# A two-layer transformer kernel on one core: its first eight heads' maxima ahead of the pipeline, its last FFN blocks inside the last attention, and GpSimd's residual sums in later steps

## The chip, the core and the metric

The kernel runs on one core of a Trainium2 chip. The metric is the device time of one execution in microseconds (us); lower is better. Five engines work side by side: TensorE (PE, whose weight loads are listed as PEld), VectorE (DVE), ScalarE (ACT), GpSimd (POOL) and SyncE (SP), which here only issues transfers. Each runs its own instruction stream in order, and waits on semaphores that the others raise.

## What is computed

Eight sequences of 256 tokens with width 128 pass two post-norm layers, all in float32:

```python
x = _layernorm(x + _L0_attn_ref(x, Wqkv, bqkv, Wproj, bproj))        # 16 heads of 8, no mask
x = _layernorm(x + _L0_ffn_ref(x, W_exp, ..., down_bias))            # 128 -> 512, butterflies, GELU, 512 -> 128
x = _layernorm(x + _L1_attn_ref(x, Wqa, Wqb, Wkva, Wkvb, Wout, bout))  # 16 heads, 4 key heads, RoPE, causal
x = _layernorm(x + _L1_ffn_ref(x, w_gate, w_up, w_down))             # SiLU-gated, 384 hidden
```

The softmax is taken over 256 keys for each of 256 queries, with the row's maximum subtracted. The butterflies of the first FFN are linear, so the kernel folds them into its two weight matrices once, at the start.

## The kernel before

**Work and numbering.** A batch b is one sequence in one layer: 0 to 7 are the first layer, 8 to 15 the second. Each has 16 heads, so there are 256 heads, m = 16 b + h. All engines walk the same list of steps g = -44, -42, ... 298, two heads a step, and each does in step g what the table of offsets at the top of the file gives it (`AT_PROJ = 26` means: batch b's projection is in step 16 b + 26). The order on every engine is thus fixed by these numbers and by the order of the `if`s in the loop body; nothing is scheduled at run time.

**One head.** A head's scores are computed twice. First `max_scores` (L342) writes queries by keys into one of three PSUM banks `SM`, and DVE takes each row's negative maximum into `mx` (L708; L716 with the mask in the second layer). Every eight heads PE transposes `mx` (L415), ACT copies it to `mt` (L587), and a transfer (L269) puts it into row 31 of the query operand `QK`, whose key side has a row of ones. Then `exp_scores` (L361) computes keys by queries, with the maximum already subtracted, into one of three banks `ST`, and ACT writes the exponentials to `E` (L580). `max_scores` runs `LEAD = 14` heads ahead of `exp_scores`. A head uses 31 or 32 rows of the array; the four strips of 32 rows can work at once. From step -8 to -2 `filler` (L372) takes the place of `exp_scores`.

**The start.** Six matmuls on zeros (L392) come first. Batch 0's operands are made straight into strips by four groups of matmuls (L406, a group r for heads 4r to 4r+3, queries and keys in one of two banks `G`), which ACT copies out with the bias (L610). The groups are in steps -44, -12, -8 and -4 (`FIRST_AT`). Batch 1 is projected in step -10 (L498), copied by ACT (L620), and split into strips by four transfers, issued by ACT's own queue (L626); all later batches' strips are issued by SP (L285). GpSimd builds the folded FFN weights meanwhile (L847 to L864), adds the projection's bias to the residual `xb` (L939), and goes on with the folding.

**The middle.** In a batch's steps follow: values times `E` (L524), DVE's transpose (L805) and reciprocal (L726), GpSimd's product (L885), DVE's transpose (L731), the projection (L468), the residual sum and statistics (L790, L674, L677), GpSimd's LayerNorm (`normalise`: L831, L827, L828, L834), and PE's transpose of its result (L475) into `xt`. In the first layer GpSimd adds the next bias to the normalised tile right behind it, to make the next residual (L916); the same follows the FFN's LayerNorm, for tiles of two batches (L924). The FFN of the first layer takes tiles of two batches, that of the second single batches: `up` (L435, three chunks c), ACT's tanh (L594), DVE's two products (L751, L753), `down` (L457).

**The end.** From step 256 on there are no more scores, and PE may use all eight banks. Batch 14's FFN chunks are in steps 258, 262 and 268, its `down` in 270; batch 15's attention ends with the second half of its values in 260, the projection in 266, LayerNorm in 268 (GpSimd gives the inverse deviation, DVE the rest: L684), transpose in 272; its FFN follows in 274 to 286.

Of the kernel before, what the change touches and what calls it, by code (L numbers as in the profile page):

```python
# [82 lines left out]
def values_at(g):  # L83

    for l in range(2):
        for parity in range(2):
            b = batch_at(g, AT_V[l][parity], (l,))
            if b is not None and b % 2 == parity:
                return b
    return None  # L90
# [20 lines left out]
def block_kernel(nc, x_nat, x_t, ones, wfirst, bfirst, wqk0, wv0, bqk0, bv0, wproj, bproj, u0, d0, fac_u, fac_d, bfw, bup, bcon, bdown,  # L111
# [7 lines left out]
    with ctx:  # L119
# [80 lines left out]
        idle_ready, first_ps, first_out = sem("idle_ready"), sem("first_ps"), sem("first_out")  # L200
# [28 lines left out]
        def layer(b):  # L229
            return b // NB  # L230

# [6 lines left out]
        def _(sp):  # L238
# [26 lines left out]
            for g in STEPS:  # L265
# [7 lines left out]

                if b is not None and b != 1:
# [31 lines left out]
        def _(pe):  # L306
# [18 lines left out]

            def max_scores(m, c):
# [15 lines left out]
                ins = nc.tensor.matmul(SM[m % S_RING][:, cols], q, QK[rows, b % QK_RING, r, 1, keys], start=True, stop=True)  # L342
# [23 lines left out]
            def filler(m, c):  # L366
# [3 lines left out]
                if c == 0 and m >= S_RING - FILL:  # L370
                    pe.wait_ge(filled, m + FILL - S_RING + 1)
# [21 lines left out]

            for g in STEPS:
                scores(g)

                for r in range(GROUPS):
                    if g == FIRST_AT[r]:
                        bank = claim(("first", r), first_out, 2 * (r + 1))
                        if r == 0:  # L400
                            pe.wait_ge(ld["x0"], 16)
                            pe.wait_ge(ld["first"], 32)
                        elif r == 1:
                            pe.wait_ge(ld["groups"], 16)
                        for s in range(2):
                            ins = nc.tensor.matmul(bank[:, s * T:(s + 1) * T], wfirst_sb[:, r, s, :], xt[:, 0:T], start=True, stop=True)  # L406
                        ins.then_inc(first_ps, 1)
# [18 lines left out]
                for c in range(SC):  # L426
                    if (b := batch_at(g, AT_UP1[c], (1,))) is not None:
# [81 lines left out]
                if (n := half_at(g, AT_PV)) is not None:  # L509
# [4 lines left out]
                    else:  # L514
                        pe.wait_ge(A["masked"], 4 * (n - 2 * NB + 1))
                    if t == 0:
                        pe.wait_ge(A["v_ready"], b + 1)
                    for e in range(2):
                        for k in range(QT):
# [44 lines left out]
        def _(act):  # L564
# [5 lines left out]

            for g in STEPS:
# [16 lines left out]
                for c in range(SC):  # L588
                    if (b := batch_at(g, AT_UP1[c], (1,))) is not None:
# [13 lines left out]
                for r in range(GROUPS):  # L603
                    if g == FIRST_AT[r]:

                        act.wait_ge(first_ps, r + 1)
                        if r == 0:
                            act.wait_ge(ld["first"], 32)
                        for s in range(2):
# [470 lines left out]
```

## Time and profile before

| | us |
|---|---|
| median of 3 runs | 374.52 |
| the runs | 372.81, 374.52, 375.20 |
| the profiled execution, its own time | 375.42 |
| its span, first to last instruction | 373.5 |

The profiled execution is 0.9 us above the median, and 1.9 us of it lie outside the span. Mean granted TensorE clock: 0.965 of full speed. Busy shares of the span: PE 91%, its weight loads 63%, DVE 67%, ACT 51%, POOL 48%. PE's share is to be read with care, since matmuls overlap and their ends are modelled; its idle stretches are exact enough, and each names what ended it.

### The profile page before, as it was taken

Reading aid. Unit: us, or ns where it says so; the run is one execution under the profiler, and the core shown is the slowest. Engines: PE = TensorE matmul, PEld = TensorE weight load, DVE = VectorE, ACT = ScalarE, POOL = GpSimd, SP = SyncE. Lnnn points to the kernel's source line nnn. Section 1 sums busy time; section 2 is a strip of 40 time slices with the busy share of each in tenths; the row PEclk is TensorE's granted clock in tenths of the full one; section 3 lists DMA queues with packets and bytes.
Section 4 is the critical chain, followed back from the end, with each engine's and each line's share of the span. In section 5 each row is a group of like instructions: output and inputs, shape, how many; then the busy total and the mean of one; then the engine's idle time right before and its main releaser. Section 6 shows DMA issues by size and latency. Waiting matters only on the chain.

```text
span 373.5 us, 10260 instructions
## 1 busy us (share of the span) xinstructions
PE 340.0 (91%) x3804; PEld 234.7 (63%) x3804; DVE 250.9 (67%) x940; ACT 189.2 (51%) x397; POOL 178.1 (48%) x299
## 2 busy tenths in 40 slices
PE   7879999999999999999999699898999999999672
PEld 3546766666657656576657566586777767676452
DVE  3444667586866777586866668486888898964533
ACT  2123755745585655836575445744556555545100
POOL 5664072140300706046352967339695954637420
PEclk9696999999999999999999989999999999999968
DMA  7321522110011001200202011110112110000000
GB/s 262 125 92 66 75 71 79 31 31 2 3 32 30 4 1 31 47 16 17 46 14 44 4 31 29 33 30 3 32 45 48 29 40 10 18 3 16 16 14 14
DMA packets 9469, 14.27 MB, mean 38 GB/s; under 512 B 2140, under 2 KB 5196, under 8 KB 9292
## 3 DMA queue, kind: packets, MB, share of 16 engines
q1 hardware_dynamic: 8828, 12.83, 13.5%
q10 hardware_dynamic: 592, 0.79, 0.7%
q8 instruction: 30, 0.49, 0.5%
q14 instruction: 19, 0.16, 0.2%
HBM read 6.28 MB, written 1.05 MB: 20 GB/s over the span
## 4 chain that ended last, share of the span: by engine, by line
PE 73%; POOL 9%; issue 6%; ACT 5%; DVE 5%; ACTq 1%; POOLq 0%; DVEq 0%
PE SM L342 26%; PE G L524 10%; PE ST L361 6%; PE G L435 5%; PE G L448 4%; PE G L498 4%; PE G L424 3%; PE G L457 2%; PE G L415 2%; PE G L506 2%; POOL ln_f L834 2%; ACT L580 1%; PE G L468 1%; POOL xb L924 1%; PE ST L392 1%
## 5 line engine op out<-in xcount | busy, mean ns | idle before, releaser
L580 ACT ACTIVATE E<-ST 128x512 f32<-128x512 f32 (+1 forms) x256 | 125.3, 541 | 126.5 <-PE ST L361 126.4
L342 PE MATMUL SM<-QK 31*128 31x256 f32 (+1 forms) x1024 | 146.6, 384 | 8.0 <-ACT QK L610 4.2
L361 PE MATMUL ST<-QK 32*128 32x256 f32 (+1 forms) x1024 | 137.6, 379 | 4.4 <-ACT E L580 4.4
L342 PEld LDWEIGHTS SM<-QK 31*128 31x128 f32 x1024 | 97.7, 189 | 49.0 <-DVE mx L708 13.3
L708 DVE TENSOR_REDUCE mx<-SM 128x2 f32<-128x512 f32 x128 | 82.2, 685 | 44.0 <-PE SM L342 43.6
L361 PEld LDWEIGHTS ST<-QK 32*128 32x128 f32 x1024 | 92.1, 187 | 8.0 <-ACT E L580 6.5
L716 DVE CUSTOM_DVE_ANT_0 masked_s<-SM,mask_sb 128x256 f32<-128x256 f32 (+1 forms) x256 | 75.7, 351 | 23.9 <-PE SM L342 23.3
L885 POOL TENSOR_TENSOR at<-turned,rec 128x256 f32<-128x256 f32 x16 | 10.1, 628 | 94.9 <-DVE rec L726 94.9
L524 PE MATMUL G<-E,V 128*32 128x256 f32 x992 | 53.6, 356 | 0.5 <-POOL E L878 0.5
L878 POOL TENSOR_SCALAR_AFFINE_SELECT E<-E 128x512 f32<-128x512 f32 x64 | 39.0, 634 | 14.0 <-ACT E L580 14.0
L524 PEld LDWEIGHTS G<-E,V 128*32 128x32 f32 x992 | 28.6, 109 | 22.4 <-issue 8.0
L805 DVE STREAM_TRANSPOSE turned<-G 128x256 f32<-128x256 f32 x31 | 13.9, 449 | 16.8 <-PE G L524 16.6
L435 PE MATMUL G<-xt,wf 128*128 128x256 f32 x76 | 21.9, 412 | 0.7 <-ACT xt L599 0.6
L716 DVE DVE_READ_ACCUMULATOR2_ANT mx<- 128x1 f32 x256 | 21.2, 83 | 0.0
L424 PE MATMUL G<-xt,wup 128*128 128x512 f32 x32 | 17.3, 621 | 0.0
L448 PE MATMUL G<-down,hid 128*128 128x128 f32 x128 | 16.3, 281 | 0.1
L435 PEld LDWEIGHTS G<-xt,wf 128*128 128x128 f32 x76 | 13.4, 196 | 4.6 <-ACT xt L599 0.9
L448 PEld LDWEIGHTS G<-down,hid 128*128 128x128 f32 x128 | 15.0, 191 | 1.9 <-issue 0.7
L751 DVE SCALAR_TENSOR_TENSOR gated<-th,G 128x256 f32<-128x256 f32 x19 | 8.0, 420 | 10.0 <-ACT th L594 9.9
L834 POOL TENSOR_SCALAR ln_a<-r_a,nm_a,rstd_a 128x128 f32<-128x128 f32 x30 | 13.2, 447 | 1.6
L415 PE MATMUL G<-id,mx 128*8 128x128 f32 x64 | 12.7, 280 | 0.0
L831 POOL TENSOR_SCALAR nm_a<-mv_a 128x2 f32<-128x2 f32 x15 | 2.9, 191 | 20.2 <-DVE mv_a L677 20.2
(130 smaller groups left out, 427.5 us busy)
## 6 DMA issues: line engine op xcount, KB each, us to landing
QK<-qk SPq DMA_DIRECT2D x56, 64.0 KB
rs<-ry SPq DMA_DIRECT2D x16, 128.0 KB, 2.3
xb<-x_nat SPq DMA_DIRECT2D x1, 1024.0 KB, 4.8
out<-ln_g SPq DMA_DIRECT2D x8, 128.0 KB, 1.9
xt<-x_t SPq DMA_DIRECT2D x1, 896.0 KB, 6.7
wi<-wi_all SPq DMA_DIRECT2D x1, 576.0 KB, 3.8
QK<-mt SPq DMA_DIRECT2D x32, 8.0 KB
fac<-fac_u SPq DMA_DIRECT2D x1, 508.0 KB, 6.4
```

The lines of the kernel that those rows point to most:

```text
L342: ins = nc.tensor.matmul(SM[m % S_RING][:, cols], q, QK[rows, b % QK_RING, r, 1, keys], start=True, stop=True)
L361: ins = nc.tensor.matmul(ST[m % S_RING][:, c * T:(c + 1) * T - q0], QK[rows, b % QK_RING, r, 1, c * P:(c + 1) * P], QK[rows, b % QK_RING, ...
L415: ins = nc.tensor.transpose(bank[0:8, q * P:(q + 1) * P], mx[:, n % 2, q, :], id32[:, :])
L424: nc.tensor.matmul(bank[:, :], wup[:, c * P:(c + 1) * P], xt[:, n * FT:(n + 1) * FT], start=True, stop=True).then_inc(F0["up_ps"], 1)
L435: ins = nc.tensor.matmul(bank[:, s * T:(s + 1) * T], wf[:, s, c * P:(c + 1) * P], xt[:, i * T:(i + 1) * T], start=True, stop=True)
L448: ins = nc.tensor.matmul(bank[:, i * W:(i + 1) * W], hid0[:, c, s * P:(s + 1) * P], down[:, c, :], start=(c == 0), stop=(c == HC - 1))
L524: ins = nc.tensor.matmul(bank[VCOL * j:VCOL * (j + 1), q0:T], values, E[:, (2 * n + e) % E_RING, j, k * T:(k + 1) * T - q0], start=(e == 0 ...
L580: act.activation(E[:, a % E_RING, j, 0:n], ST[m % S_RING][:, 0:n], ACT.Exp, scale=SCALE)\
L708: ins = nc.vector.tensor_reduce(mx[:, n % 2, :, i], bank[:, :].rearrange("p (q k) -> p q k", q=QT), AX.X, ALU.max, negate=True)
L716: ins = nc.vector.tensor_tensor_reduce(out=masked_s[:, m % 2, lo:hi], in0=bank[:, lo:hi], in1=mask_sb[:, T + lo - hi:T], scale=-1.0, scala ...
L834: ins = nc.gpsimd.tensor_scalar(N["ln"][:, parity, s, :], N["r"][:, s, :], N["nm"][:, s:s + 1], N["rstd"][:, s:s + 1], ALU.add, ALU.mult)
L878: nc.gpsimd.affine_select(out=e, in_=e, pattern=[[0, 4], [1, P]], compare_op=ALU.is_ge, fill=0.0, base=0, channel_multiplier=-1).then_inc( ...
```

## The change

It does five things.

1. **Eight heads' maxima ahead of the steps.** `AHEAD = 8`: before the loop over steps PE makes groups 0 and 1, then the maxima of heads 0 to 7, four heads in a run (all their second halves, then all their first halves), then groups 2 and 3. These eight take turns in all six banks, `SM` and `ST`. Group 0's keys go to `ST2`, from where DVE adds the bias, while ACT does the queries. The steps begin at -6, not -44, and the filler has three steps.
2. **Batch 1 and the first values** move to steps -6 and -4; batch 1's strips are issued by SP like the others.
3. **Batch 14's FFN**: PE and ACT have its last chunk in step 264, not 268. DVE has its three chunks in 262, 264 and 268, not 258, 262 and 268, and there the last comes ahead of batch 15's LayerNorm.
4. **Finer waits in batch 15**: `down` starts when two of the three hidden chunks are there, and the last values start when the first of two groups of four heads is masked.
5. **GpSimd's residual sums** leave the LayerNorm: by batch from step 28 to 34 (`AT_XB`), by tile from 74 to 88 (`AT_XB0`).

```diff
+LAST_UP1, LAST_GATED = (34, 38, 40), (38, 40, 44)
+AT_XB, AT_XB0 = 34, 88
-FIRST, FINAL = AT_QK[2], HEADS + 44
+AHEAD = 2 * STRIPS
+FIRST, FINAL = AHEAD - LEAD, HEADS + 44
 STEPS = range(FIRST, FINAL, 2)
-FIRST_AT, EARLY, FILL = (FIRST, -12, -8, -4), (None, -10, 2), 8
+EARLY, EARLY_V, FILL = (None, FIRST, 2), FIRST + 2, 6
...
+def up1_at(g, c, last=LAST_UP1):
+    b = batch_at(g, AT_UP1[c], (1,))
+    return BATCHES - 2 if g - last[c] == H * (BATCHES - 2) else b if b != BATCHES - 2 else None
...
+        keys_bank = ST[S_RING - 1]
+        def max_bank(m):
+            return (SM + ST)[m % (2 * S_RING)] if m < AHEAD else SM[m % S_RING]
...
+            def project_group(r):
+                bank = claim(("first", r), first_out, 2 * r + 1)
...
+                for s in range(2):
+                    to = keys_bank if r == 0 and s == 1 else bank
+                    ins = nc.tensor.matmul(to[:, s * T:(s + 1) * T], wfirst_sb[:, r, s, :], xt[:, 0:T], start=True, stop=True)
+                ins.then_inc(first_ps, 1)
...
                     if b == 0 and j == 0:
-                        pe.wait_ge(first_out, 2 * (r + 1))
+                        pe.wait_ge(first_out, 2 * r + 1)
+                        if r == 0:
+                            pe.wait_ge(first_keys, 1)
...
-                    if m >= S_RING:
+                    if m >= AHEAD:
                         pe.wait_ge(A["max_done"], m - S_RING + 1)
+                    elif m >= 2 * S_RING:
+                        pe.wait_ge(A["max_done"], m - 2 * S_RING + 1)
...
+            project_group(0)
+            project_group(1)
+            for r in range(2):
+                for c in (1, 0):
+                    for m in range(STRIPS * r, STRIPS * (r + 1)):
+                        max_scores(m, c)
+            project_group(2)
+            project_group(3)
...
-                    pe.wait_ge(F1["hid_ready"], SC * (i + 1))
+                    pe.wait_ge(F1["hid_ready"], SC * (i + 1) - (1 if b == BATCHES - 1 else 0))
                     for q in range(QT):
                         for c in range(SC):
+                            if q == 0 and c == SC - 1 and b == BATCHES - 1:
+                                pe.wait_ge(F1["hid_ready"], SC * (i + 1))
...
-                        if b == 1:
-                            act.wait_ge(A["qk_out"], 2)
-                            act.wait_ge(zeros_ready, 1)
-                            for j in range(STRIPS):
-                                act.dma_start(QK[STRIP * j:STRIP * j + ROWS, 1, :, :, :], qk[j:P:STRIPS, 1, :, :]).then_inc(qk_in[1], 16)
...
+            dve.wait_ge(first_ps, 1)
+            dve.wait_ge(ld["first"], 32)
+            nc.vector.tensor_scalar(QK[:, 0, 0, 1, :], keys_bank[:, T:2 * T], bfirst_sb[:, 0, 1:2], None, ALU.add)\
+                .then_inc(first_keys, 1)
+            for m in range(AHEAD):
+                maximum(m)
...
-                    if (b := batch_at(g, AT_UP1[c], (1,))) is not None:
+                    if (b := up1_at(g, c, LAST_GATED)) is not None:
...
+                if g == H * (BATCHES - 1) + AT_LN:
...
+                    normalise_last(NA, b % 2, A["ln_ready"])
...
-                    if layer(b) == 0:
-                        pool.wait_ge(A["ln_ready"], b + 1)
+                if (b := batch_at(g, AT_XB, (0,))) is not None:
+                    pool.wait_ge(A["ln_ready"], b + 1)
...
                     normalise(N0, FS, n % 2, F0["ln_ready"])
+                if (n := tile_at(g, AT_XB0)) is not None:
                     pool.wait_ge(F0["ln_ready"], n + 1)
```

Line numbers in the rows below are those of the file they are from; a row with x2 stands for two instructions of one kind in sequence.

PE at the start, before (groups L406, maxima L342, filler L372, batch 1 L498, transposed maxima L415):

```order
L392 MATMUL ST<-idle 128x512 x3
L406 MATMUL G<-xt,wfirst_sb 128x256 x2
L342 MATMUL SM<-QK 128x256 x8
L406 MATMUL G<-xt,wfirst_sb 128x256 x2
L342 MATMUL SM<-QK 128x256 x4
L498 MATMUL G<-xt,wqk_sb 128x256 x2
...
L406 MATMUL G<-xt,wfirst_sb 128x256 x2
L506 MATMUL G<-wv_sb,xt 128x128 x2
...
L415 MATMUL G<-id,mx 8x128 x2
```

and with the change (groups L356, maxima L379, filler L412, batch 1 L537):

```order
L432 MATMUL ST<-idle 128x512 x3
L356 MATMUL G<-xt,wfirst_sb 128x256
L356 MATMUL ST<-xt,wfirst_sb 128x256
L356 MATMUL G<-xt,wfirst_sb 128x256 x2
L379 MATMUL SM<-QK 128x256 x3
L379 MATMUL ST<-QK 128x256
...
L356 MATMUL G<-xt,wfirst_sb 128x256 x4
L379 MATMUL SM<-QK 128x256 x2
L412 MATMUL ST<-QK 128x256 x2
...
L452 MATMUL G<-id,mx 8x128 x2
L537 MATMUL G<-xt,wqk_sb 128x256 x2
```

All four groups now come before the first filler, the eight heads' maxima stand between the first two and the last two, and batch 1 is behind the transposed maxima instead of ahead of them.

GpSimd at the first tile's LayerNorm, before:

```order
L834 TENSOR_SCALAR ln_f<-r_f,nm_f,rstd_f 128x128 x4
L924 TENSOR_TENSOR xb<-ln_f,bout_sb 128x512
L831 TENSOR_SCALAR nm_a<-mv_a 128x2
L827 TENSOR_SCALAR ve_a<-mv_a 128x2
L828 TENSOR_TENSOR rstd_a<-ve_a,half 128x2
L834 TENSOR_SCALAR ln_a<-r_a,nm_a,rstd_a 128x128 x2
```

and with the change:

```order
L881 TENSOR_SCALAR ln_f<-r_f,nm_f,rstd_f 128x128 x4
L878 TENSOR_SCALAR nm_a<-mv_a 128x2
L874 TENSOR_SCALAR ve_a<-mv_a 128x2
L875 TENSOR_TENSOR rstd_a<-ve_a,half 128x2
L881 TENSOR_SCALAR ln_a<-r_a,nm_a,rstd_a 128x128 x2
L963 TENSOR_TENSOR xb<-ln_a,bcon_sb 128x256
L932 TENSOR_TENSOR at<-turned,rec 128x256
L972 TENSOR_TENSOR xb<-ln_f,bout_sb 128x512
```

The sum of 128x512 has left the place between the two LayerNorms.

DVE from the last values on, before:

```order
L751 SCALAR_TENSOR_TENSOR gated<-th,SM 128x256
L753 TENSOR_TENSOR hid<-SM,gated 128x256
L731 STREAM_TRANSPOSE att<-at 128x256
L790 TENSOR_TENSOR r_a<-ST,xb 128x256
L674 BN_STATS stats_a<-r_a 128x6 x2
L677 BN_AGGR mv_a<-stats_a 128x2 x2
L684 TENSOR_SCALAR ln_a<-r_a,mv_a,rstd_a 128x128 x2
L751 SCALAR_TENSOR_TENSOR gated<-th,ST 128x256
L753 TENSOR_TENSOR hid<-ST,gated 128x256
```

and with the change:

```order
L777 STREAM_TRANSPOSE att<-at 128x256
L797 SCALAR_TENSOR_TENSOR gated<-th,SM 128x256
L799 TENSOR_TENSOR hid<-SM,gated 128x256
L842 TENSOR_TENSOR r_a<-ST,xb 128x256
L710 BN_STATS stats_a<-r_a 128x6 x2
L713 BN_AGGR mv_a<-stats_a 128x2 x2
L797 SCALAR_TENSOR_TENSOR gated<-th,ST 128x256
L799 TENSOR_TENSOR hid<-ST,gated 128x256
L720 TENSOR_SCALAR ln_a<-r_a,mv_a,rstd_a 128x128 x2
```

One pair of products moved behind the transpose `att`, another ahead of `ln_a`. On PE the last chunk's matmuls (before L435 into `ST`) moved ahead of the projection (L468).

## Rows read from the trace of the kernel before

**Rows 1.** Stretches in us: length, then each engine's busy time (instructions), granted clock, DMA.

```profile
12.90:19.60 6.70, 6.23 (x29) 3.78 (x30) 1.40 (x3) 1.25 (x4) 6.20 (x10) 0.50 0.01 3
29.90:36.70 6.80, 6.80 (x41) 4.20 (x38) 3.14 (x7) 2.81 (x7) 4.20 (x1) 0.50 0.00 0
214.20:217.70 3.50, 3.46 (x24) 2.69 (x24) 0.53 (x3) 1.51 (x5) 3.42 (x3) 0.51 0.00 0
357.60:364.40 6.80, 6.24 (x20) 5.07 (x20) 2.00 (x7) 1.15 (x3) 1.96 (x5) 0.50 0.06 19
```

**Rows 2.** PE's timeline, 0 to 46 us: start, length, operation, [idle before <- what ended it].

```profile
22.47 0.48 PE L342 MATMUL SM<-QK 31*128 31x256 f32 x2 [1.39 <-ACT QK L610]
...
23.54 0.38 PE L415 MATMUL G<-id,mx 128*8 128x128 f32 x2
...
31.95 0.80 PE L342 MATMUL SM<-QK 31*128 31x256 f32 x2
...
37.49 1.13 PE L498 MATMUL G<-xt,wqk_sb 128*128 128x256 f32 x4
...
40.72 0.67 PE L342 MATMUL SM<-QK 31*128 31x256 f32 x2
```

**Rows 3.** The timelines of DVE, ACT, SP and GpSimd at the start.

```profile
9.51 1.29 DVE L708 TENSOR_REDUCE mx<-SM 128x2 f32<-128x512 f32 x2 [4.46 <-PE SM L342]
...
7.45 0.84 ACT L610 ACTIVATE QK<-G,bfirst_sb 128x256 f32<-128x256 f32 x2 [3.75 <-PE G L406]
...
18.36 3.17 ACTq L626 DMA_DIRECT2D QK<-qk  x4
...
37.17 2.64 SPq L285 DMA_DIRECT2D QK<-qk  x4
...
32.50 4.51 POOL L939 TENSOR_TENSOR xb<-xb,bproj_sb 128x2048 f32<-128x2048 f32 x1 [7.09 <-DVE bproj_sb L814]
...
59.21 0.63 POOL L885 TENSOR_TENSOR at<-turned,rec 128x256 f32<-128x256 f32 x1 [3.01 <-DVE rec L726]
```

**Rows 4.** DMA activity from 17 to 25 us, in 40 slices of 0.2 us.

```profile
DMA  0000000000000243000433333146300003000000
```

**Rows 5.** GpSimd's sums for the residual, all four tiles and all eight batches.

```profile
L924 POOL TENSOR_TENSOR xb<-ln_f,bout_sb x4: 1264/1266/1273, 124.7 to 254.1; 128x512 f32<-128x512 f32 x4
...
L916 POOL TENSOR_TENSOR xb<-ln_a,bcon_sb x8: 722/730/737, 66.2 to 213.4; 128x256 f32<-128x256 f32 x8
```

**Rows 6.** PE's waits between 46 and 340 us: total us, times, longest.

```profile
PE G L475 <- POOL ln_a L834: 4.8, 4, 2.8
```

**Rows 7.** PE's timeline at the last two of those four waits.

```profile
213.45 0.41 PE L475 MATMUL G<-id,ln_a 128*128 128x128 f32 x2 [2.80 <-POOL ln_a L834]
...
258.91 0.41 PE L475 MATMUL G<-id,ln_a 128*128 128x128 f32 x2 [1.08 <-POOL ln_a L834]
```

**Rows 8.** The page's groups: GpSimd's idle time before its product for the attention.

```profile
L885 POOL TENSOR_TENSOR at<-turned,rec 128x256 f32<-128x256 f32 x16 | 10.1, 628 | 94.9 <-DVE rec L726 94.9
```

**Rows 9.** PE's timeline at the end.

```profile
352.33 0.68 PE L468 MATMUL ST<-wout_sb,att 128*128 128x128 f32 x4 [1.83 <-DVE att L731]
...
356.90 2.31 PE L457 MATMUL ST<-wf,hid 128*128 128x128 f32 x12 [3.02 <-DVE hid L753]
...
366.57 1.57 PE L457 MATMUL SM<-wf,hid 128*128 128x128 f32 x12 [1.48 <-DVE hid L753]
```

**Rows 10.** DVE's timeline at the end.

```profile
350.95 0.42 DVE L751 SCALAR_TENSOR_TENSOR gated<-th,SM 128x256 f32<-128x256 f32 x1 [0.61 <-ACT th L594]
...
351.75 0.43 DVE L731 STREAM_TRANSPOSE att<-at 128x256 f32<-128x256 f32 x1
353.05 0.42 DVE L790 TENSOR_TENSOR r_a<-ST,xb 128x256 f32<-128x256 f32 x1 [0.87 <-PE ST L468]
...
355.37 0.60 DVE L684 TENSOR_SCALAR ln_a<-r_a,mv_a,rstd_a 128x128 f32<-128x128 f32 x2 [1.09 <-POOL rstd_a L828]
...
368.18 0.42 DVE L773 TENSOR_TENSOR r_g<-SM,ln_a 128x256 f32<-128x256 f32 x1 [1.76 <-PE SM L457]
```

More of the change, by code:

```diff
@@ L83, in values_at @@
 def values_at(g):
+    if g == EARLY_V:
+        return 0
     for l in range(2):
@@ L87, in values_at @@
             b = batch_at(g, AT_V[l][parity], (l,))
-            if b is not None and b % 2 == parity:
+            if b and b % 2 == parity:
                 return b
@@ L272, in _ @@
                     b = batch_at(g, AT_QKIN, (1,))
-                if b is not None and b != 1:
+                if b is not None:
                     if layer(b) == 0:
@@ L324, in claim @@
                 return banks[i]
+            def project_group(r):
+                bank = claim(("first", r), first_out, 2 * r + 1)
+                if r == 0:
+                    pe.wait_ge(ld["x0"], 16)
+                    pe.wait_ge(ld["first"], 32)
+                elif r == 1:
+                    pe.wait_ge(ld["groups"], 16)
+                for s in range(2):
+                    to = keys_bank if r == 0 and s == 1 else bank
+                    ins = nc.tensor.matmul(to[:, s * T:(s + 1) * T], wfirst_sb[:, r, s, :], xt[:, 0:T], start=True, stop=True)
+                ins.then_inc(first_ps, 1)
             def max_scores(m, c):
@@ L341, in max_scores @@
                     cols, keys = (slice(T, T + P), slice(0, P)) if c == 0 else (slice(0, T), slice(0, T))
-                ins = nc.tensor.matmul(SM[m % S_RING][:, cols], q, QK[rows, b % QK_RING, r, 1, keys], start=True, stop=True)
+                ins = nc.tensor.matmul(max_bank(m)[:, cols], q, QK[rows, b % QK_RING, r, 1, keys], start=True, stop=True)
                 if c == 0:
@@ L426, in _ @@
                 for c in range(SC):
-                    if (b := batch_at(g, AT_UP1[c], (1,))) is not None:
+                    if (b := up1_at(g, c)) is not None:
                         i = b - NB
@@ L518, in _ @@
                     for e in range(2):
+                        if e == 1 and n == 2 * BATCHES - 1:
+                            pe.wait_ge(A["masked"], 4 * (n - 2 * NB + 1))
                         for k in range(QT):
@@ L569, in _ @@
             act.activation(warm[:, :], half[:, 0:1], ACT.Exp).then_inc(act_chain, 1)
+            for r in range(GROUPS):
+                act.wait_ge(first_ps, r + 1)
+                if r == 0:
+                    act.wait_ge(ld["first"], 32)
+                for s in range(1 if r == 0 else 2):
+                    act.activation(QK[:, 0, r, s, :], g_bank["first", r][:, s * T:(s + 1) * T], ACT.Identity,
+                                   bias=bfirst_sb[:, r, s:s + 1]).then_inc(first_out, 1)
             for g in STEPS:
@@ L588, in _ @@
                 for c in range(SC):
-                    if (b := batch_at(g, AT_UP1[c], (1,))) is not None:
+                    if (b := up1_at(g, c)) is not None:
                         i = SC * (b - NB) + c
@@ L602, in _ @@
                     act.activation(xt[:, n * FT:(n + 1) * FT], g_bank["xt0", n][:, :], ACT.Copy).then_inc(F0["xt_ready"], 1)
[L603 to L609, printed above, removed]
-                            act.activation(QK[:, 0, r, s, :], g_bank["first", r][:, s * T:(s + 1) * T], ACT.Identity,
-                                           bias=bfirst_sb[:, r, s:s + 1]).then_inc(first_out, 1)
                 if (b := projected_at(g)) is not None:
@@ L694, in _, with maximum @@
                 ins.then_inc(v_clean, 1)
+            def maximum(m):
+                b, r, j = place(m)
+                n = m // 8
+                i = 2 * j + r % 2
+                dve.wait_ge(A["sm_ps"], m + 1)
+                if m % 8 == 0 and n >= 2:
+                    dve.wait_ge(A["mt_ps"], n - 1)
+                bank = max_bank(m)
+                if layer(b) == 0:
+                    ins = nc.vector.tensor_reduce(mx[:, n % 2, :, i], bank[:, :].rearrange("p (q k) -> p q k", q=QT),
+                                                  AX.X, ALU.max, negate=True)
+                else:
+                    if m == NB * H:
+                        dve.wait_ge(ld["rope"], 48)
+                    if m >= NB * H + 2:
+                        dve.wait_ge(A["max_done"], m - 1)
+                    for q, lo, hi in ((1, 0, T), (0, T, T + P)):
+                        ins = nc.vector.tensor_tensor_reduce(
+                            out=masked_s[:, m % 2, lo:hi], in0=bank[:, lo:hi], in1=mask_sb[:, T + lo - hi:T], scale=-1.0,
+                            scalar=3.0e38, op0=ALU.add, op1=ALU.min, accum_out=mx[:, n % 2, q, i:i + 1])
+                ins.then_inc(A["max_done"], 1)
@@ L719, in _ @@
-                    ins.then_inc(A["max_done"], 1)
+                    if m < HEADS:
+                        maximum(m)
                 if (b := batch_at(g, AT_NORM)) is not None:
```

64 lines of the change are left out of this document (17 added, 47 removed).

## The prediction

> **What bounds the kernel.** I read the clock by stretches first, then each engine's timeline at both ends, then PE's waits in the middle. PE is busy for 91% of the span, and between 46 and 340 us it hardly waits, so a microsecond comes off only where PE idles or runs at half clock, or where work is taken from its stream. The granted clock is at its lower level (0.50, 1.2 GHz) in four stretches, 23.8 us together [rows 1]: two at the start, one at 214 us, one at the end. Each follows a time in which PE kept stopping: the one at 214 us stands right behind the wait of 2.80 us [rows 7], the last behind waits of 1.83 and 3.02 us [rows 9]. In the middle PE's largest wait is for GpSimd's `ln_a`, 4.8 us in four places [rows 6].
>
> **The front end.** Before, the first operands begin to leave PSUM at 7.45, the first maximum starts at 9.51 [rows 3], the first eight maxima are transposed only at 23.54, step 2 starts at 31.95 and step 8 at 40.72 [rows 2]. What spreads this out is order: four groups, each followed by a round trip through ACT, in four different steps.
> Now with the change, at full clock:
> - Group 1 follows group 0 at once. Two matmuls of 256 columns on the full array take 1.07 us (37.49 with 1.13, less the overlap) [rows 2], so PE is free for maxima at 8.5. That ACT and DVE share group 0's copies saves half of 0.84 [rows 3], but PE doesn't get there before 8.5, so it is worth nothing.
> - A step's eight score matmuls over four strips take 1.07 (22.47 to 23.54) [rows 2]. Sixteen, in runs of four strips, take 2.1; the first head is whole at about 9.4. DVE's two maxima take 1.29 [rows 3], so eight take 5.2: the last ends at 14.6. Groups 2 and 3 (2.1) and ACT's copies lie under that. PE makes step -6's scores meanwhile and transposes the maxima at about 14.9, 8.6 earlier than before.
> - Batch 1: its two matmuls end at 16.3, ACT's copies at 17.2 (0.84). PE goes on with three steps' scores (3.2), the values (0.5) and the bias product (0.4), and stands before step 2 at 20.4. **Here is a new wait.** Step 2 begins with batch 1's first maxima, hence with its strips. SP needs 2.64 for four issues [rows 3], so the last ends at 19.85. In the trace ACT's last issue ended at 21.53 [rows 3] and the activity of these transfers at about 22.8 [rows 4]: 1.3 later. So the strips are there at 21.15; PE waits 0.75 and all of its queue with it. Before, this was hidden: 22.8 against a use at 31.95.
>
> The Trainium skill ("DMA: Bandwidth & Descriptors", the two cost components of a transfer) states a fixed cost of about 2.0 us instead; by it the strips would land at 21.85 and the front end would gain 0.7 less.
>
> - So step 2 starts at 21.2 instead of 31.95. From step 2 to 8 the old kernel needed 8.77, of which 4.75 at half clock (until 36.70 [rows 1]); at full clock 6.4. Step 8 would start at 27.6: **13.1 earlier**.
> - But PE still stops (for the copies, for DVE, for the strips), and half clock came twice in this part of the old trace, 6.7 and 6.8 us long [rows 1]. A stretch costs half its length, 3.3. None gives 13.1, one 9.8, two 6.5. I take one: the stops are fewer, not gone.
> - What else must keep pace? GpSimd's folding ran until 25.4 and then idled 7.09 for `bproj` [rows 3]; that now comes at about 21, so its 4.5 us sum starts at 25.4, 7.1 earlier. At batch 0's product it waited another 3.01 [rows 3]. Together 10.1 us of slack for a shift of 9.8. SP's loads are tied to the steps and move along. I count nothing, with 0 to 3 us as bounds.
>
> **GpSimd's sums.** Four sums of 1.27 and eight of 0.73 [rows 5] move, 10.9 us. The former stood just ahead of `ln_a`. PE's waits behind them are 4.8 in all, of them 2.80 and 1.08 in the last two places [rows 6, 7], so 0.92 in the first two. A sum less takes up to 1.27 from each: 0.92 + 1.27 + 1.08 = 3.3. At 213 us 1.5 of the wait stays. Then the half-clock stretch of 3.5 us behind it [rows 1] should go too, half its length, 1.7, since waits no longer than 1.5 stand elsewhere in the middle (PE's other stops) without one. Together **5.0**; bounds 2.5 (half of the waits come back as waits for ACT or DVE, which catch up while PE stands, and the stretch stays at about half its worth) and 5.2. The moved sums are free where they land: GpSimd waits 94.9 us before its sixteen products [rows 8], and the tiles' sums come in the step behind such a product. Without that cover the price would be their 10.9 us at most.
>
> **The end.** Before: `att` waits until 351.75 because the products of chunk 1 (0.42 each) stand ahead of it; projection 352.33; LayerNorm's first sum 353.05; `ln_a` at 355.37 after 1.09 of waiting for GpSimd; then chunk 2's products; `down` at 356.90 [rows 9, 10]. Now:
> - DVE does chunk 0's products while GpSimd makes its product (0.63 [rows 8]), so `att` starts at 351.3, 0.45 earlier, and the projection 0.45 earlier too, at 351.9; PE has made chunk 2 by then. Chunk 1's products (0.87) follow `att` and end at 352.65; the sum starts there, 0.4 earlier than 353.05.
> - From the sum to `ln_a` it is 2.32 as before, the last 1.09 of it GpSimd's [rows 10]: from 353.9 to 355.0. Chunk 2's products (0.87) now fill that, so the hidden chunks are complete at 354.8, and `down` starts at 354.95 instead of 356.90: 1.95.
> - Batch 15's `down` begins with two of its six matmuls (1.57 for all six [rows 9]) ahead of the last chunk: 0.5.
> - The split wait on the masks: PE does not wait for them at the last values. Nothing.
>
> So 2.5 at the clock of before. If PE stays at full clock, `down` and the four matmul pairs behind it take about 2.5 less again (half clock from 357.6 on [rows 1]): 5.0. Before, 1.83 and 3.02 of idle time stood ahead of the fall; now 0.4 and 2.4. The nearest row is the 2.80 that was followed by a fall at 214 us, so I take **2.5**; bounds 2.0 and 5.3.
>
> **Sum.** 9.8 + 5.0 + 2.5 = 17.3 off the profiled execution's 375.42 gives 358.1. That execution stood 0.9 above the median of 374.52, so I forecast a median of **357.2**. The ends of all terms together: 13.1 + 5.2 + 5.3 = 23.6 (350.9), and 6.5 + 2.5 + 2.0 - 3 for GpSimd = 8.0 (366.5).
>
> **Rivals.**
> - *Full clock throughout* (chance 0.15): no half-clock stretch at the start, none at the end. 13.1 + 5.0 + 5.0 = 23.1, so 351.4. For it: PE's runs are longer and of four strips. Against it: the waits of 0.75 and 2.4.
> - *The clock falls as often as before* (0.12): two stretches at the start: 6.5 + 5.0 + 2.5 = 14.0, so 360.5.
> - *The sums don't pay* (0.1): PE's waits at `ln_a` turn into waits for ACT's exponentials or DVE's maxima, and the stretch at 214 us stays: 9.8 + 0.5 + 2.5 = 12.8, so 361.7. Against it: DVE and ACT are busy 67% and 51%.
> - *The front end only moves its wait* (0.07): GpSimd's folding, or the loads that SP issues between steps, hold PE at steps 4 to 26, and only the 3.01 of slack of batch 0's product [rows 3] is gained: 3.0 + 5.0 + 2.5 = 10.5, so 364.0.
> - *Slower than before* (0.015): the clock. If PE, started with short bursts, were kept at the lower level beyond step 8 through the first batches, each us would cost half a us. To eat the 17.3 it would have to last 35 us longer than the one stretch that I count, 41 in all; 50 us would give 4.4 more than before, 378.9. No stretch in the trace lasts more than 6.8 [rows 1].
>
> My forecast has 0.53, and its own range is 354.5 to 359.5. The range 351.5 to 362.5 leaves out about half of the full-clock case, most of the held front end, and the slower one. What this kernel's runs can tell from no change is about 1% (3.7 us). Faster by more than that: all cases but the last and a mishap of several parts, 0.965; within 1%: 0.02; slower: 0.015.
>
> **What would show it.** In the changed kernel's profile: the eight maxima's transpose at 15 rather than 23.5; a PE wait of about 0.75 ahead of step 2 with the transfer of `QK` as its cause; step 8 at 31 (28 if the clock stays up); one half-clock stretch before 45 us and none near 200; PE's waits for `ln_a` at 1.5 to 2 us in all; GpSimd still waiting for DVE before its products; at the end, batch 14's `down` 3.1 us after the start of the last projection (before: 352.33 to 356.90, 4.6). It is wrong if step 2 starts after 25, if new PE waits for GpSimd's masks appear in the second layer, or if half clock holds for longer than 10 us at the start.

## The result, and the profile after

| | before | changed |
|---|---|---|
| median, us | 374.59 (4 runs) | 358.67 (4 runs) |
| the runs | 372.81 to 375.20 | 358.60 to 360.17 |
| profiled execution, own time | 375.42 | 358.65 |
| its span | 373.5 | 356.5 |
| mean granted clock | 0.965 | 0.989 |

The ratio is 0.9592, with a 95% interval of 0.9551 to 0.9633: faster by 4.1%. The forecast was 357.2, in a range of 351.5 to 362.5. The sum was near; its three terms were not, and the rest of this part is about them.

Two points cut both traces alike: the start of step 8, and the start of the first half of batch 15's values (`L524`, now `L565`, the first of the last two such groups).

| stretch of the span | before | changed | gain | forecast |
|---|---|---|---|---|
| start to step 8 | 40.72 | 32.41 | 8.3 | 9.8 |
| step 8 to batch 15's values | 301.50 | 298.73 | 2.8 | 5.0 |
| from there to the end | 31.28 | 25.36 | 5.9 | 2.5 |

The page of the changed kernel, its clock in tenths of full speed over 40 slices, and its stretches at the lower level and at the end:

```profile
PEclk9989999999999999999999999989999999999999
```

```profile
24.30:27.80 3.50, 3.50 (x21) 2.40 (x22) 1.29 (x2) 1.33 (x3) 2.24 (x2) 0.51 0.52 201
232.50:236.00 3.50, 3.50 (x17) 3.32 (x16) 1.59 (x7) 0.62 (x2) 1.80 (x3) 0.51 0.35 80
343.40:350.00 6.60, 5.31 (x30) 4.30 (x30) 4.26 (x13) 1.53 (x4) 2.17 (x6) 1.00 0.07 22
```

Two stretches, 7 us in all, in place of four with 23.8 [rows 1]. The one at 214 is gone, but there is another at 232.5, and the end runs at full clock.

**The start.** PE's timeline, answering to [rows 2]:

```profile
15.55 0.38 PE L452 MATMUL G<-id,mx 128*8 128x128 f32 x2
...
20.36 0.48 PE L379 MATMUL SM<-QK 31*128 31x256 f32 x1 [0.15 <-DVE mx L742]
...
21.80 0.46 PE L575 MATMUL G<-wproj_sb,bv_all 128*128 128x128 f32 x2 [0.20 <-issue]
24.22 0.70 PE L379 MATMUL SM<-QK 31*128 31x256 f32 x2 [1.96 <-DMA QK<-qk]
...
32.41 0.67 PE L379 MATMUL SM<-QK 31*128 31x256 f32 x2
```

and DVE's, ACT's and SP's, answering to [rows 3]:

```profile
10.02 1.89 DVE L742 TENSOR_REDUCE mx<-SM 128x2 f32<-128x512 f32 x3 [1.44 <-PE ST L379]
...
19.61 1.29 DVE L742 TENSOR_REDUCE mx<-SM 128x2 f32<-128x512 f32 x2 [0.43 <-PE SM L379]
20.82 0.88 DVE L858 TENSOR_SCALAR bv_all<-id,bv_sb 128x128 f32<-128x128 f32 x1
...
8.10 0.47 ACT L618 ACTIVATE QK<-G,bfirst_sb 128x256 f32<-128x256 f32 x1 [4.41 <-PE ST L356]
...
17.70 2.65 SPq L304 DMA_DIRECT2D QK<-qk  x4
```

The maxima are transposed at 15.55 (forecast 14.9). Most of that lateness comes from ahead of the first group: the six matmuls on zeros, the same in both kernels, took 5.49 in this execution and 5.05 in the one of before, so group 0 began at 6.78 against 6.39. (Counted from there to step 8, the gain is 8.7.) The new wait ahead of step 2 is there, with the cause that was forecast, but it is 1.96 long instead of 0.75, although PE came to it at 22.26 instead of 20.4. SP's last issue ended at 20.35; PE went on behind the strips at 24.22, 3.9 us later, not 1.3.

**The middle.** PE's waits between 30 and 325 us, the largest, and three places of its timeline:

```profile
PE ST L398 <- ACT E L630: 3.8, 4, 1.5
PE SM L379 <- DVE mx L750: 1.9, 4, 0.6
PE G L514 <- POOL ln_a L881: 1.4, 1, 1.4
...
PE G L545 <- ACT xt L649: 0.5, 1, 0.5
```

```profile
202.76 0.41 PE L514 MATMUL G<-id,ln_a 128*128 128x128 f32 x2 [1.44 <-POOL ln_a L881]
...
231.03 0.48 PE L398 MATMUL ST<-QK 32*128 32x256 f32 x1 [1.50 <-ACT E L630]
...
249.17 0.71 PE L545 MATMUL G<-wl,xt 128*128 128x128 f32 x4 [0.50 <-ACT xt L649]
```

Of four waits for `ln_a` with 4.8 us [rows 6] one is left, with 1.4. The last place got a new one of 0.5 right behind: what was late next is ACT's copy of the transposed tile. The wait of 1.50 for ACT (a GELU between two table loads) was there before too, also with 1.5; this time the clock fell behind it.

**The end.** PE's and DVE's timelines, answering to [rows 9, 10]:

```profile
331.14 1.51 PE L565 MATMUL G<-E,V 128*32 128x256 f32 x32
...
340.60 0.68 PE L507 MATMUL ST<-wout_sb,att 128*128 128x128 f32 x4 [0.32 <-DVE att L777]
343.46 1.58 PE L496 MATMUL ST<-wf,hid 128*128 128x128 f32 x12 [2.18 <-DVE hid L799]
...
349.26 1.93 PE L496 MATMUL SM<-wf,hid 128*128 128x128 f32 x12 [0.61 <-DVE hid L799]
```

```profile
343.64 0.60 DVE L720 TENSOR_SCALAR ln_a<-r_a,mv_a,rstd_a 128x128 f32<-128x128 f32 x2 [0.33 <-POOL rstd_a L875]
...
351.23 0.42 DVE L825 TENSOR_TENSOR r_g<-SM,ln_a 128x256 f32<-128x256 f32 x1 [1.25 <-PE SM L496]
```

The projection's matmuls and `down` start 2.86 apart (before 4.57 [rows 9]; forecast 3.1). Batch 15's `down` begins ahead of its last chunk, and DVE waits 1.25 for it instead of 1.76 [rows 10]: the half microsecond of the forecast. And `down` of batch 14 takes 1.58, not 2.31: the clock stayed up.

### The profile page after: what moved, and what is told of

It reads as the page before. It is cut to its first block, busy times and chain, and to the rows that moved or that the text cites. A ratio compares the mean times of both kernels' runs of the same rounds, so it can differ in the third digit from the quotient of the medians.

```text
span 356.5 us, 10245 instructions
## 1 busy us (share of the span) xinstructions
PE 331.8 (93%) x3796; PEld 230.5 (65%) x3796; DVE 251.3 (70%) x941; ACT 188.5 (53%) x396; POOL 177.8 (50%) x299
## 4 chain that ended last, share of the span: by engine, by line
PE 76%; issue 7%; POOL 6%; ACT 5%; DVE 4%; DMA 1%; SPq 1%; POOLq 0%; DVEq 0%; ACTq 0%
PE SM L379 28%; PE G L565 12%; PE ST L398 5%; PE G L472 5%; PE G L485 5%; PE G L537 3%; PE G L461 3%; PE G L452 2%; PE G L545 2%; PE G L496 2%; POOL E L925 2%; PE G L507 2%; PE ST L432 2%; ACT L630 1%; ACT E L630 1%
## 5 line engine op out<-in xcount | busy, mean ns | idle before, releaser
L379 PE MATMUL SM<-QK 31*128 31x256 f32 (+1 forms) x1012 | 141.2, 377 | 5.1 <-DMA QK<-qk 2.0
L398 PE MATMUL ST<-QK 32*128 32x256 f32 (+1 forms) x1024 | 136.0, 376 | 4.4 <-ACT E L630 4.4
L379 PEld LDWEIGHTS SM<-QK 31*128 31x128 f32 x1012 | 94.7, 185 | 44.0 <-DVE mx L742 12.3
L742 DVE TENSOR_REDUCE mx<-SM 128x2 f32<-128x512 f32 x125 | 80.2, 684 | 31.8 <-PE SM L379 30.0
L398 PEld LDWEIGHTS ST<-QK 32*128 32x128 f32 x1024 | 91.0, 185 | 8.0 <-ACT E L630 6.5
L565 PE MATMUL G<-E,V 128*32 128x256 f32 x992 | 53.6, 356 | 0.5 <-POOL E L925 0.5
L565 PEld LDWEIGHTS G<-E,V 128*32 128x32 f32 x992 | 28.7, 110 | 22.3 <-issue 8.1
L750 DVE DVE_READ_ACCUMULATOR2_ANT mx<- 128x1 f32 x256 | 21.2, 83 | 0.0
L485 PEld LDWEIGHTS G<-down,hid 128*128 128x128 f32 x128 | 16.5, 207 | 2.1 <-issue 0.7
L485 PE MATMUL G<-down,hid 128*128 128x128 f32 x128 | 17.7, 296 | 0.1
L786 DVE TENSOR_SCALAR hid<-G,bhid 128x512 f32<-128x512 f32 x16 | 11.6, 725 | 1.0 <-PE G L461 0.8
```

What stands on the lines that cost most here:

```text
L379: ins = nc.tensor.matmul(max_bank(m)[:, cols], q, QK[rows, b % QK_RING, r, 1, keys], start=True, stop=True)
L398: ins = nc.tensor.matmul(ST[m % S_RING][:, c * T:(c + 1) * T - q0], QK[rows, b % QK_RING, r, 1, c * P:(c + 1) * P], QK[rows, b % QK_RING, ...
L485: ins = nc.tensor.matmul(bank[:, i * W:(i + 1) * W], hid0[:, c, s * P:(s + 1) * P], down[:, c, :], start=(c == 0), stop=(c == HC - 1))
L565: ins = nc.tensor.matmul(bank[VCOL * j:VCOL * (j + 1), q0:T], values, E[:, (2 * n + e) % E_RING, j, k * T:(k + 1) * T - q0], start=(e == 0 ...
L742: ins = nc.vector.tensor_reduce(mx[:, n % 2, :, i], bank[:, :].rearrange("p (q k) -> p q k", q=QT), AX.X, ALU.max, negate=True)
L750: ins = nc.vector.tensor_tensor_reduce(out=masked_s[:, m % 2, lo:hi], in0=bank[:, lo:hi], in1=mask_sb[:, T + lo - hi:T], scale=-1.0, scala ...
```

## The experiments

Ratios are to the kernel before on the same chip, with 95% intervals. The first four ran together, as did the next four and the last four.

| run | median, us | ratio | interval |
|---|---|---|---|
| changed kernel | 358.67 | 0.9592 | 0.9551 to 0.9633 |
| e1 front end alone | 366.61 | 0.9806 | 0.9751 to 0.9861 |
| e2 sums back | 363.97 | 0.9708 | 0.9662 to 0.9753 |
| e3 end back | 364.14 | 0.9726 | 0.9683 to 0.9769 |
| e4 residual loaded early | 359.23 | 0.9592 | 0.9551 to 0.9634 |
| e5 loads held | 358.79 | 0.9576 | 0.9532 to 0.9621 |
| e6 strips from two queues | 359.76 | 0.9606 | 0.9561 to 0.9651 |
| e7 start kept warm | 356.28 | 0.9511 | 0.9472 to 0.9549 |
| e8 old end kept warm | 362.49 | 0.9673 | 0.9634 to 0.9712 |
| e9 start kept warm, again | 356.50 | 0.9518 | 0.9487 to 0.9550 |
| e10 = e9, sums back | 363.94 | 0.9707 | 0.9672 to 0.9742 |
| e11 = e9, split waits back | 357.56 | 0.9551 | 0.9516 to 0.9586 |
| e12 = e9, one more in the middle | 361.51 | 0.9644 | 0.9612 to 0.9676 |

### e1, e2, e3: one part at a time

```diff
 e1: all three edits below
 e2:
-AT_XB, AT_XB0 = 34, 88
+AT_XB, AT_XB0 = AT_LN, AT_LN0
 e3:
-LAST_UP1, LAST_GATED = (34, 38, 40), (38, 40, 44)
+LAST_UP1, LAST_GATED = AT_UP1, AT_UP1
-                if g == H * (BATCHES - 1) + AT_LN:          # ln_a behind the last chunk's products
...
+                    if b == BATCHES - 1:                    # ln_a in the projection's step
...
-                    pe.wait_ge(F1["hid_ready"], SC * (i + 1) - (1 if b == BATCHES - 1 else 0))
+                    pe.wait_ge(F1["hid_ready"], SC * (i + 1))
-                        pe.wait_ge(A["masked"], 4 * (n - 2 * NB + 1) - (2 if n == 2 * BATCHES - 1 else 0))
+                        pe.wait_ge(A["masked"], 4 * (n - 2 * NB + 1))
```

> The changed kernel with its residual sums back in steps 28 and 74 and its end as before: the front end alone differs from the kernel before. If the parts add up as the two traces suggest (8.3 us of the span up to step 8), this runs at 374.6 - 8.3 = 366.3. If part of the front end's gain is given back later, because GpSimd's folding or SP's loads no longer keep ahead of the steps, it is above 368.

> The changed kernel with GpSimd's residual sums back directly behind the LayerNorms. If the sums' place is worth what the waits for ln_a show (4.8 before, 1.4 after: 3.4, less a new wait of 0.5 for xt), this runs at 358.7 + 2.9 = 361.6, with four waits for ln_a again. The rival: PE's queue catches up elsewhere, and it is 359.0 to 360.0.

> The changed kernel with the old end: batch 14's third chunk in step 268, its products in 258, 262, 268 behind LayerNorm, and no split waits. Theory 1, the order is worth 2.5 and the clock the rest: the granted clock falls again ahead of batch 14's down, and it runs at 358.7 + 5.9 = 364.6. Theory 2, the clock at the end has nothing to do with the order (it depends on how the executions happen to fall): the clock stays at full speed, and it is 361.2.

e1 ran at 366.6, 8.5 below the 375.15 of the kernel before beside it (by the interval, 5.2 to 9.3). So the front end's 8.3 are kept, as far as that interval can tell, and in the middle PE waits for GpSimd, ACT and DVE about as long as before (4.9 against 4.8 for `ln_a`); the 1.3 that its trace gives back between step 8 and batch 15's values goes with one more half-clock stretch there, at 332. Of the ratio's 4.1%, the front end alone has 1.9; putting the sums back costs 1.2 (e2), putting the end back 1.3 (e3), and both together 2.1 (e1). That 1.2 and 1.3 are not quite 2.1 lies within the intervals, which reach 0.4 to 0.6 to either side.

e2 came out well above both theories: PE's waits for `ln_a` are 4.8 again, which is 2.9 with the new wait of 0.5 taken off. The rest fits the clock: its six executions had mean granted clocks of 0.975 to 0.980, the changed kernel's four 0.980 to 0.989. e3 met the first theory's 364.6. Its trace has the clock fall again near the end, and `down` of batch 14 slow behind the old wait:

```profile
346.11 2.90 PE L494 MATMUL ST<-wf,hid 128*128 128x128 f32 x12 [3.03 <-DVE hid L795]
```

Over all traces this `down` was slow (2.20 to 2.90 instead of 1.58) in three of three with the old end (before, e1, e3), and in four of ten with the new one (e2, e10, e11, e12). So the new order does not rule the fall out; that it makes it rarer is suggested by so few traces, not shown.

### e4, e5: why the strips land late

```diff
 e4:
-                     (ld["bf"], facs[1][:, :, :], fac_d), (ld["bf"], bup_sb[:, :], bup)]
+                     (ld["bf"], facs[1][:, :, :], fac_d), (ld["bf"], bup_sb[:, :], bup), (ld["xb"], xb[:, :, :], x_nat)]
...
 e5:
+                if g == LATE:
+                    sp.wait_ge(qk_in[1], 16 * STRIPS)
                 if 0 <= (i := (g - LATE) // 2) < len(late):
```

> The changed kernel with the 1 MB load of the residual (xb) moved from behind batch 1's strips to the end of SP's first loads, so that it moves at 9 to 16 us. Theory 1, the strips land 3.8 us after their last issue because that load shares the DMA engines with them: they land at about 21.7, PE's wait ahead of step 2 goes from 2.0 to under 0.3, and the time is 356.9, or 355.4 if the half-clock stretch at 24.6 to 27.6 goes too. Theory 2, strips issued by SP need that long by themselves: the wait stays at about 2 us and the time at 358.7.

> The changed kernel, but SP issues the residual's load and all loads behind it only once batch 1's strips have landed. Nothing else is then on the DMA engines. Theory 1, the 512-byte pieces of the two bias loads behind the strips slow their landing: PE's wait ahead of step 2 shrinks from 2.0 to 0.5 or less. Theory 2, a strip transfer raises its semaphore a fixed 1.9 us after its last packet whatever else runs (in the two traces so far the last 2 KB packets were over by 22.2, PE was released at 24.1): the wait stays at 2.0, and the time at 358.7 to 359.5.

In both, the first theory fell. PE's wait for the strips in e4; then, for e5, SP's issue, the DMA activity from 16 to 24 us in 40 slices of 0.2, and PE's wait:

```profile
24.22 0.64 PE L380 MATMUL SM<-QK 31*128 31x256 f32 x2 [1.98 <-DMA QK<-qk]
```

```profile
17.38 2.65 SPq L304 DMA_DIRECT2D QK<-qk  x4
```

```profile
DMA  0000001000020433225046554564100000000000
```

```profile
23.59 0.74 PE L381 MATMUL SM<-QK 31*128 31x256 f32 x2 [1.90 <-DMA QK<-qk]
```

With no other load on the engines PE goes on at 23.59, 3.6 after the last issue ended (20.03), and the last packet is over by 21.8. In the changed kernel the last 2 KB packets of the strips run at about 22.2 (by the count of packets by size in half microseconds), and PE goes on at 24.22. So in the last 1.8 to 2.0 a strip transfer shows no packet; this time lies between its last packet and its semaphore. The Trainium skill ("DMA: Bandwidth & Descriptors", where the fixed 2 us go), of transfers that GpSimd issues, says that most of a fixed 2.0 us is the confirmation that the data has landed. This case's rows, of transfers that SP issues, agree with that part. But the whole, from the end of the last issue, is 3.6 to 3.9 here, since the packets of four transfers, issued 0.66 apart, run on until 1.8 after the last issue.

### e6: two queues

```diff
-                    for j in range(STRIPS):
+                    for j in range(2 if b == 1 else STRIPS):      # SP
...
+                        if b == 1:                                # ACT, behind its two copies
...
+                            for j in range(2, STRIPS):
+                                act.dma_start(QK[STRIP * j:STRIP * j + ROWS, 1, :, :, :], qk[j:P:STRIPS, 1, :, :]).then_inc(qk_in[1], 16)
```

> The changed kernel with batch 1's four strips issued by two queues, two by SP and two by ACT. If the wait is issue time in a row plus a fixed landing time, the last issue ends 1.3 us earlier and PE's wait goes from 2.0 to 0.7; the time falls by 1.3 to 357.4, or by up to 2.9 if the half-clock stretch behind the wait (24.6 to 27.6) goes too. The rival: the packets of both queues share the engines and land no earlier; the wait stays near 2.0.

Worse: PE's wait grew to 3.4. SP's and ACT's issues, and PE behind them:

```profile
17.33 1.35 SPq L304 DMA_DIRECT2D QK<-qk  x2
18.73 0.45 SPq L316 DMA_DIRECT2D xb<-x_nat  x1
```

```profile
17.33 2.17 ACTq L667 DMA_DIRECT2D QK<-qk  x2
```

```profile
25.76 0.80 PE L379 MATMUL SM<-QK 31*128 31x256 f32 x2 [3.37 <-DMA QK<-qk]
```

The issues took 2.17 from first to last instead of 2.65 (this execution's whole start is 0.37 earlier). SP's two took 1.35, no longer than two of its four elsewhere; ACT's first took 1.52 and its second 0.62. ACT's first is slow without a second queue too: in the kernel before, where ACT issued all four alone, they took 1.22 and then 0.62 to 0.63 each. So by these two traces issuing at once cost ACT 0.3. And with two strips less to issue SP reached the 1 MB load at 18.7, while ACT was still issuing; the strips came at 25.7. A large load behind the strips in the same queue costs them nothing (e4); one that is issued before the last of them seems to, though no run separates it from the change of queue.

### e7, e9: the clock behind the wait

```diff
+                if g == BV:
+                    bank = claim("idle", idle_ready, 1)
+                    for _ in range(2):
+                        nc.tensor.matmul(bank[:, :], idle[:, 0:P], idle[:, :], start=True, stop=True)
```

> The changed kernel with two matmuls of 512 columns on zeros (0.85 us each at full clock) on PE in step 0, just ahead of the wait for the strips; their results are read by nobody. If the wait is what lets the clock fall at 24.6, the stretch goes and step 8 starts 1.5 us earlier: 357.2. If the clock falls for the sum of smaller stops before, or at random, it stays: 358.7 or, if they outlast the wait, more.

> The changed kernel with the two matmuls on zeros in step 0, once more, as the base of the three runs beside it on the same chip. It repeats 356.3 within 0.5, and 2.4 ahead of the changed kernel's 358.7; if the gain was luck in how the clock fell, it is back at 358.7.

With two matmuls that nobody reads, put into a wait, the kernel ran at 356.28 against 358.67, ratio 0.9511 against 0.9592; the repeat gives 356.50 and 0.9518. PE in e7, and the clock from 23 to 30 us in e9:

```profile
21.18 1.88 PE L579 MATMUL G<-idle 128*128 128x512 f32 x4
23.54 0.48 PE L379 MATMUL SM<-QK 31*128 31x256 f32 x2 [0.48 <-DMA QK<-qk]
...
30.10 0.67 PE L379 MATMUL SM<-QK 31*128 31x256 f32 x2
```

```profile
23.00:30.00 7.00, 7.00 (x73) 5.19 (x77) 3.70 (x6) 5.18 (x13) 6.82 (x4) 1.00 0.40 127
```

From step 2 to step 8 it is 6.56 instead of 8.19, near the 6.4 of the forecast at full clock. The half-clock stretch right behind the wait for the strips stands in all eight traces that have this wait and no fill (the changed kernel, e1 to e6, e8), 3.5 or 6.8 us long, and in none of the five with the fill (e7, e9 to e12). That shows what the fill does.

What it wins is less sure than 2.4. Step 2 itself starts 0.68 sooner in e7's trace than in the changed kernel's (23.54 against 24.22), and 1.34 sooner in e9's, for a reason that has nothing to do with the fill: the six matmuls on zeros at the very start. In the changed kernel's trace, then in e9's:

```profile
1.50 5.49 PE L432 MATMUL ST<-idle 128*128 128x512 f32 x6 [1.50 <-DVE idle L716]
```

```profile
1.50 4.23 PE L432 MATMUL ST<-idle 128*128 128x512 f32 x6 [1.50 <-DVE idle L720]
```

Over all traces they took 4.23 to 5.49, in e7 5.02 with the very code of e9, so executions of one kernel can differ there by 0.8. The fill's own part, read from the traces, is 1.6 (8.19 to 6.56); the other 0.5 to 0.8 between the medians can be this start, or stretches of 6.8 instead of 3.5 in other executions, and no run separates them. Nor is all of the clock kept: e7's trace has a stretch at 200 that the changed kernel's has not, behind a wait of 1.44.

This is the fastest version: the upper ends of its two intervals, 0.9549 and 0.9550, lie just under the lower end of the changed kernel's, 0.9551.

### e8: how much of the end is order, how much clock

```diff
 as e3, and
+                if g in (LAST_WAIT, LAST_WAIT + 2):              # steps 266 and 268
+                    bank = claim(("idle", g), idle_ready, 1, g)
+                    for _ in range(1 if g == LAST_WAIT else 2):
+                        nc.tensor.matmul(bank[:, :], idle[:, 0:P], idle[:, :], start=True, stop=True)
```

> The changed kernel with the old order at the end (as in the run with the old end), and three matmuls of 512 columns on zeros in PE's two stops there (one ahead of the last projection, two ahead of batch 14's down). If the order is worth 2.5 and the clock the rest, the clock stays up and this runs 2.5 to 3 behind the changed kernel, 361.3 to 361.7, against 364.1 for the old end without them. If the clock falls all the same, it is 364.

```profile
331.56 1.51 PE L566 MATMUL G<-E,V 128*32 128x256 f32 x32
...
346.24 1.58 PE L495 MATMUL G<-wf,hid 128*128 128x128 f32 x12 [1.31 <-DVE hid L800]
```

The clock stayed up at the end, and from batch 15's values to the end of the span (359.8) it is 28.24. With the new order it is 25.36, with the old order and the fall of the clock 31.28. So order and split waits are worth 2.9, the clock 3.0. The median of 362.5 is about 1 above what I expected, of which 0.4 is the order's 2.9 instead of 2.5; the rest fits the clock ahead of the end, where this trace has 6.8 us of half clock behind the wait for the strips and 3.5 at 202, the changed kernel's 3.5 and none.

### e10, e11, e12: on the warm start

```diff
 e10: AT_XB, AT_XB0 = AT_LN, AT_LN0
 e11: the two split waits of batch 15 as in the kernel before
 e12:
+                if g == BV or tile_at(g, AT_GELU + 2) == NF - 1:
...
+                    for _ in range(2 if g == BV else 1):
```

> The same with GpSimd's residual sums back behind the LayerNorms. With the clock at the start held up, what is left is the sums and what their waits do to the clock. If the sums' place is worth its waits alone, this is 2.9 behind: 359.2. If the wait of 2.8 also lets the clock fall each time and nothing falls in its place, it is 4.6 behind: 360.9.

> The same with the two split waits of batch 15 made whole again (its down waits for all three hidden chunks, its last values for both groups of heads). In the changed kernel's trace the sum after this down starts 1.25 after the last chunk, before 1.76: so 0.5 slower, 356.8. If the last values' split wait also matters, 1 slower.

> The same with one more matmul on zeros (0.85 us) on PE in step 164, in the stop of 1.5 us behind which the clock fell at 232 in the changed kernel. If that stop is what lets it fall, 1.7 us are won: 354.6. If the clock falls elsewhere instead, or the extra matmul's bank holds up what follows, 356.3 to 357.

**e10**: 363.9, 7.4 behind e9, more than both theories. The waits for `ln_a` are 4.8 against 1.4, as in e2. The rest is clock: e9's trace has one stretch, near 231; e10's has none there, but these three.

```profile
200.00:207.50 7.50, 4.70 (x42) 3.84 (x35) 1.40 (x11) 2.31 (x6) 7.08 (x11) 0.58 0.00 0
332.00:338.80 6.80, 6.80 (x51) 4.34 (x51) 1.29 (x3) 1.92 (x5) 2.14 (x6) 0.57 0.05 17
346.00:352.00 6.00, 3.38 (x15) 3.04 (x15) 3.35 (x13) 0.38 (x1) 1.65 (x4) 0.72 0.07 22
```

The first begins in the middle of the 2.80 wait for `ln_a`. The second stands behind a wait of 0.57 for ACT, which e9 has in the same place, at full clock, and the third in the new order's wait of 2.2, at which the clock stayed up in the changed kernel and in e9. So whether half clock follows a stop is not decided by that stop alone. Not even the kernel decides it: e7 and e9 are the same code, and the wait of 1.44 for `ln_a` was followed by half clock in e7's execution and not in e9's. What decides it no run here shows.

One trace against one exaggerates, since e9's was its fastest execution. Over all six of each, the mean granted clock is 0.990 in e9 and 0.978 in e10. That is an average of 7 us at the lower level against 16, and since half of that time is lost, an estimated 4.5; with the 2.9 of waits it makes the 7.4.

**e11**: 357.6, 1.1 behind e9, with overlapping intervals. In the trace the sum behind the last `down` waits 1.76 for it again, against 1.25: the 0.5 of the split. The rest can't be told from noise.

**e12**: 361.5, 5 slower. The matmul took a bank whose reader was late, and PE waited for it:

```profile
PE G L579 <- ACT ry L670: 3.0, 1, 3.0
```

The bank belongs to batch projections that ACT copies (`ry`) behind the GELU's table load; the wait of 1.5 became one of 3.0 in an earlier place, ahead of score matmuls that could have run. But this is not where the trace loses most. PE's wait for `hid` ahead of the fill ends 2.21 later than in e9 (220.79 against 218.58), and the values at 305.11 behind it start 2.54 later (e9: 302.57). So across the fill only 0.3 is lost: the longer wait and the matmul, less the half-clock stretch that e9 has there and e12 has not. Of the 2.21, 2.0 come from a half-clock stretch of 6.8 at 199, ahead of the fill, and from the last values on another 1.4 are lost, with a stretch of 3.5 at 342. The trace is thus 3.9 behind in its span, mostly by falls of the clock elsewhere; how the medians' 5.0 divide is not shown, nor what a fill without a claim would win there.

## Why the prediction came out

The mechanisms were right: a shorter start, a new wait for strips ahead of step 2, waits for `ln_a` gone but for 1.5, `down` brought forward. Three wrong sizes cancelled, and that is luck: the front end gained 1.5 less than forecast, the middle 2.2 less, the end 3.4 more, so 17.0 in all against 17.3. The time was 1.5 off, and most of that is in none of the three: I took 0.9 off because the profiled execution of before stood that far above its median, while the changed kernel's stood at its median (358.65 against 358.67). The other 0.6 are the 0.3 of the terms and 0.2 more outside the span.

- **The landing of the strips, off by 2.5.** I took the end of DMA activity [rows 4] for the landing. It is the last packet; PE went on 1.8 to 2.0 later (e5 and the changed kernel). By the 2.0 that the Trainium skill ("DMA: Bandwidth & Descriptors", the two cost components) states, counted from the end of the issue, the wait would have been 1.4, still too short. Before, nothing waited there, so no row could show it; I should have given this term an upper bound, from transfers that somebody waits for.
- **PE's way to step 2, 1.9 late**, hidden behind the strips. 0.65 of it is no effect of the change: the first operands left PSUM at 8.10 instead of 7.45 since the matmuls on zeros were slow in this execution; in e9 they left at 6.63. Another 1.1 is step 0, which took 2.2 (19.62 to 21.80) and not PE's 1.07, because its second head waited for a bank that DVE had to free (the wait at 20.36). I had counted DVE's maxima for the eight heads, but not for the six heads of steps -4 to 0 behind them.
- **The start's clock, counted too dear.** One stretch was right in number, but it was 3.5 long and cost 1.8 (step 2 to 8: 8.19 against 6.4), not 3.3. In sum 13.1 - 3.0 (step 2 at 24.2 instead of 21.2: the landing's 2.5, and 0.5 for SP's issues, which started that much later) - 1.8 = 8.3.
- **GpSimd's sums**: waits fell by 3.4 (forecast 3.3), with 0.5 back for `xt`. The 1.7 for the stretch at 214 did come, but another opened at 232.5: 2.8 between the two cuts instead of 5.0. This term can't be given as one number: with the sums back e10's trace has three falls of the clock against one, and the medians put the sums' place at 7.4 there, and at 5.3 without the fill (e2).
- **The end**: the order gave 2.9 (forecast 2.5). I chose the lower clock because a wait of 2.8 had been followed by it; it stayed up, 3.0 more. With the same order it fell in the traces of e2, e10, e11 and e12, so the choice was between two things that both occur.
- **GpSimd's cover at the start** held: e1's 8.5 is the whole of the front end's gain, within its interval.

## What to carry to other kernels

Cut both traces at the same points and compare term by term; a sum that fits may hide terms that don't. A transfer whose landing nobody waits for shows only its packets; before something is made to wait for it, add the time from last packet to semaphore. In this kernel, which PE bounds, a stop costs its length and sometimes half clock for 3.5 to 6.8 us behind it. A stop that can't be removed was worth filling where the fill's bank was free (e7), and won nothing where it had to wait for a bank (e12). And where executions of one kernel differ by 0.8 us at the start (e7, e9) and by whole half-clock stretches later, compare medians and mean clocks over several executions, not two traces alone.

## What the runs showed that was not expected

- Four 64 KB transfers between parts of SBUF, issued one behind another in 2.65 us, are complete 3.6 to 3.9 us after the last issue ended, of which 1.8 to 2.0 without a packet; a 1 MB load behind them in the same queue changes nothing (1.98 and 1.96 of waiting).
- The first such transfer that ACT issued took 1.22, the three behind it 0.62 to 0.63 each (kernel before); with SP issuing at the same time the first took 1.52, and SP's own two were no slower, 1.35 (e6).
- The same stop of 0.57, 1.44, 1.5 or 2.2 us was followed by half clock in some traces and not in others; for the 1.44, in two executions of one kernel (e7 and e9).
- The first six matmuls took 4.23 to 5.49 us in different executions, while the granted clock is shown as 1.00.
